# Graph build of a four-layer GNN and FFN kernel: part sums taken as rows in one float32 product, side work written between the tiles, and a new tail of l1_ffn

## Time and profile before

| What | us |
|---|---|
| median of 3 runs | 3308.21 (3299.77 to 3309.79) |
| the profiled execution | 3304.56 |
| its span | 3302.6 |
| build_graph's table | 0 to 29 |
| window loop of build_graph | 29 to 442 |
| finish_graph | 442 to 471 |
| end of l1_ffn, from L497 on | 1844.7 to 1884.2 |
| TensorE matmuls busy | 2694.3 (82%) |
| VectorE busy | 1684.6 (51%) |

### The profile page before, as it was taken

How to read it: one execution, slowest core, us unless ns; L and a number is a source line. 1 busy time by engine, 2 the same in 40 slices (tenths; PEclk the granted TensorE clock), 3 DMA queues, 4 the chain that set the end, 5 groups by cost and what they waited for, 6 DMA issues and landing times. The chain is left out here.

```text
span 3302.6 us, 41258 instructions
## 1 busy us (share of the span) xinstructions
PE 2694.3 (82%) x12659; PEld 1893.4 (57%) x12660; DVE 1684.6 (51%) x3356; ACT 943.7 (29%) x2087; POOL 278.1 (8%) x273
## 2 busy tenths in 40 slices
PE   5888869995899985999588599977877579999774
PEld 3555545564687754666365266665644457777452
DVE  6777752134788835444533722242132458886343
ACT  1222230103567741111111022211111236777110
POOL 0000000000000001444000000002210000000031
PEclk9999979997899987999798799978978789999777
DMA  3000042202000005898413130033232110000354
GB/s 104 1 0 0 0 135 46 60 0 63 19 19 22 16 9 168 293 301 285 114 46 129 27 75 13 0 109 112 90 91 52 44 34 19 19 18 13 81 143 110
DMA packets 113512, 237.85 MB, mean 72 GB/s; under 512 B 32500, under 2 KB 33860, under 8 KB 112130
## 3 DMA queue, kind: packets, MB, share of 16 engines
q10 hardware_dynamic: 41158, 110.67, 11.8%
q1 hardware_dynamic: 47932, 97.96, 9.9%
q0 software_dynamic: 24320, 27.90, 2.9%
HBM read 189.78 MB, written 52.58 MB: 73 GB/s over the span
## 5 line engine op out<-in xcount | busy, mean ns | idle before, releaser
L1050 DVE TENSOR_REDUCE mx<-ps 125x1 f32<-125x500 f32 (+1 forms) x480 | 273.9, 589 | 56.6 <-PE ps L820 40.4
L243 PE MATMUL ps<-onehot_src,onehot_dst 125*128 x1200 | 258.4, 354 | 41.5 <-DVE onehot_dst L219 17.4
L945 ACT ACTIVATE probs_hi<-ps 125x500 fp32r<-125x500 f32 (+1 forms) x480 | 255.7, 533 | 124.2 <-DVE probs_lo L1002 76.9
L218 DVE TENSOR_SCALAR onehot_src<-iota,src_f 125x1250 f16 x400 | 218.1, 545 | 108.1 <-PE ps L243 95.1
L1002 DVE TENSOR_TENSOR probs_lo<-x,probs_hi 125x1250 fp32r<-125x1250 f32 x160 | 240.8, 1505 | 35.7 <-ACT x L947 32.1
L947 ACT ACTIVATE x<-ps 125x500 f32<-125x500 f32 (+1 forms) x480 | 258.9, 539 | 0.0
L1694 DVE COPY yb<-ps 78x512 f32<-78x512 f32 (+1 forms) x100 | 68.9, 689 | 323.2 <-PE ps L1631 323.2
L243 PEld LDWEIGHTS ps<-onehot_src,onehot_dst 125*128 x1200 | 121.0, 102 | 172.4 <-issue 117.8
L1631 PE MATMUL ps<-w2s,hT 128*78 128x512 f32 (+1 forms) x480 | 216.7, 598 | 1.8 <-ACT hT L1656 1.8
L820 PE MATMUL ps<-K_hi_lo,Q_hi_twice 128*125 128x500 f32 (+1 forms) x480 | 181.2, 384 | 23.2 <-DVE mx L1050 18.1
L828 PE MATMUL ps<-Q_hi_twice,K_hi_lo 128*125 128x500 f32 (+1 forms) x480 | 179.5, 374 | 17.9 <-ACT Q_lo_max L935 5.1
(11 more groups left out here) (368 smaller groups left out, 4773.6 us busy)
## 6 DMA issues: line engine op xcount, KB each, us to landing
room<-in_L_ffn_w_p ACTq DMA_DIRECT2D x63, 512.0 KB, 4.7
w2s<-in_L_ffn_w ACTq DMA_DIRECT2D x63, 512.0 KB, 6.0
G<-c_spill ACTq DMA_DIRECT2D x2, 5859.4 KB
tv<-in_L_ffn_tv_W_p SPq DMA_DIRECT2D x2, 4096.0 KB
w_spill<-W SPq DMA_DIRECT2D x5, 1171.9 KB
c_spill<-CT ACTq DMA_DIRECT2D x1, 5859.4 KB
slabs<-w_spill SPq DMA_DIRECT2D x10, 585.9 KB
w1s<-in_L_ffn_w_p ACTq DMA_DIRECT2D x5, 1024.0 KB, 4.9
```

The costliest lines, as they stand in the source:

```text
L218: v.tensor_scalar(ohs[:, slot, :].rearrange("p o n -> p (o n)"), io16[:, 0:N], sF[:, bass.ds(tile, 1)], None, ALU.is_equal)
L243: mm_ = pe.matmul(ps[:, 3 * half + c, 0:cn], ohd[:, slot, :].rearrange("p o n -> p (o n)"), ohs[:, slot, c0:c0 + cn].rearrange("p o n -> p ...
L945: act.activation(PH[:, t % 2, c0:c0 + cn], ps[0:P, ST + n, 0:cn], ACT.Exp, scale=SCALE).then_inc(p_hi, 1)
L1050: v.tensor_reduce(mx[:, t, n:n + 1], ps[0:P, SQ + cc % 2, 0:cn], AX.X, ALU.max)\
```

## The change

1. HEAD = 7 tiles of each window are written out; then come runs of RUN = 2. With the same edges a window takes 9 or 11 tiles, 380 in all.
2. `sel_parts` becomes the stationary operand and `parts` (the old `stage`) the moving one: three float32 matmuls for a window (500, 500, 250 columns) give the rows of counts (partitions 0 to 31) and of weights (32 to 63) of the window. ScalarE copies them to `Crow` and `Wrow`, with the row sums of the counts as a by-product (`accum_out`, to `deg`). They stand between the written-out tiles two windows later, behind tiles 0, 2 and 4.
3. Per group ten PE transposes turn `Crow` into columns of CT, behind tiles of the next group's windows 2 and 3. ScalarE issues the write of `Wrow` to `w_spill` for each group.
4. The loop is written as a first group, a loop of 4 rounds with two groups each, and a last group; then the rest of the side work.
5. finish_graph goes; a small block works out the degree columns from `deg`.
6. In l1_ffn VectorE adds b2b to xn beside columns_product too; a new `blend` multiplies the identity with xn into the same PSUM sums, takes statistics, scales and adds to x row tile by row tile, and takes the statistics of x, so that l2_gnn's norm_rows need not.

```diff
-RUN = 4
-ETP = ET + RUN
+HEAD = 7
+RUN = 2
+ETP = ET + HEAD + RUN
...
-        stage = sb("stage", [128, 2, N])
+        parts = sb("parts", [128, 2, N])
+        Crow, Wrow = (sb(n, [P, 2, N]) for n in ("count_rows", "weight_rows"))
+        deg = sb("deg", [P, 3, T])
...
+                s.did(v.tensor_scalar(ti[:, 0:1], tl[:, 5:6], float(HEAD), float(RUN - 1 - HEAD), ALU.max, ALU.add))
...
+        AUX = 6
+        SRC = ((0, 4), (4, 4), (8, 2))
+        def sums(j, those):
+            return [("sum", j, c) for c in those]
+        def turns(*those):
+            return [("turn", None, q) for q in those]
+        def three_sums(w, n, j):
+            return {(w, 2 * c): (n + c, sums(j, (c,))) for c in range(3)}
+        PIECES = {"first": {**three_sums(2, 0, 0), **three_sums(3, 3, 1)},
+                  "body": {**three_sums(0, 0, 2), **three_sums(1, 3, 3), **three_sums(2, 6, 0), **three_sums(3, 10, 1),
+                           (2, 6): (9, turns(0)), (3, 5): (13, turns(1)), (3, 6): (14, turns(2))},
+                  "end": {(0, 0): (0, sums(2, (0, 1, 2)) + sums(3, (0, 1, 2)) + turns(0, 1, 2))}}
+        ROWS_DONE = 5
+        def chunk(i, where, n):
+            return n if where == "first" else i * 15 + (n - 9)
+        def aux(i, parity, where, q, j, slot, do_sum, do_turn):
+            first, pieces = PIECES[where].get((j, slot), (0, ()))
+            for n, (what, jj, c) in enumerate(pieces, first):
+                m, bank = chunk(i, where, n), (n + (1 if where != "first" and parity == 0 else 0)) % 2
+                if what == "turn":
+                    do_turn(i, 1 - parity, where, m, bank, c)
+                elif jj >= 2:
+                    do_sum(i - 1, jj, 1 - parity, None, m, bank, c)
+                else:
+                    do_sum(i, jj, parity, q, m, bank, c)
+        def schedule(eng, group):
+            group(0, 0, "first", 0)
+            with eng.Fori(0, T // 2 - 1) as q:
+                group(q * 2 + 1, 1, "body", q)
+                group(q * 2 + 2, 0, "body", q + 1)
+            group(T - 1, 1, "body", T // 2 - 1)
...
+                        for t in range(HEAD):
+                            onehots(first + t, before + t, base)
+                        with v.Fori(0, runs) as r:
                             for h in range(RUN):
-                                onehots(first + RUN * q + (1 + h), before + RUN * q + (1 + h), base)
+                                onehots(first + RUN * r + (HEAD + h), before + RUN * r + (HEAD + h), base)
...
+                def sum_parts(g, j, parity, q, m, bank, c):
+                    (c0, cn), h = CH[c], j % 2
+                    pe.wait_ge(aux_out, m * 2 + 2)
+                    if c == 0:
+                        pe.wait_ge(parts_ready, (g * WPT + j) * 2 + 6)
+                    pe.matmul(ps[0:64, AUX + bank, 0:cn], sel[:, :], parts[:, h, c0:c0 + cn], start=True, stop=True)\
+                        .then_inc(aux_done, 1)
+                def turn_counts(i, parity, where, m, bank, c):
+                    s0, sn = SRC[c]
+                    pe.wait_ge(aux_out, m * 2 + 2)
+                    if c == 0:
+                        pe.wait_ge(aux_out, chunk(i, where, ROWS_DONE) * 2 + 6)
+                    for t in range(sn):
+                        mm_ = pe.transpose(ps[0:P, AUX + bank, P * t:P * t + P],
+                                           Crow[:, parity, P * (s0 + t):P * (s0 + t) + P], k.ident[0:P, 0:P])
+                    mm_.then_inc(aux_done, 1)
+                def group(i, parity, where, q):
                     for j in range(WPT):
                         w = i * WPT + j
                         first, runs, before = window(pe, w)
...
+                        pe.wait_ge(parts_ready, w * 2 + 2)
+                        for t in range(HEAD):
+                            add_tile(j % 2, before + t, t == 0)
+                            aux(i, parity, where, q, j, t, sum_parts, turn_counts)
+                        with pe.Fori(0, runs) as r:
                             for h in range(RUN):
...
+                                add_tile(j % 2, before + RUN * r + (HEAD + h), False)
                         pe.drain().then_inc(window_summed, 1)
...
+                schedule(pe, group)
+                aux(T, 0, "end", None, 0, 0, sum_parts, turn_counts)
...
+                def stage_window(i, j, where):
+                    h = j % 2
                     act.wait_ge(window_summed, i * WPT + j + 1)
...
+                    if where != "first" or j >= 2:
+                        last = {0: 2, 1: 5, 2: 8, 3: 12} if where != "first" else {2: 2, 3: 5}
+                        act.wait_ge(aux_done, chunk(i, where, last[j]) + 1)
+                    act.activation(parts[:, h, 0:1000].rearrange("p (c n) -> p c n", c=2),
+                                   ps[:, 3 * h:3 * h + 2, 0:500], ACT.Copy).then_inc(parts_ready, 1)
+                    act.activation(parts[:, h, 1000:N], ps[:, 3 * h + 2, 0:250], ACT.Copy).then_inc(parts_ready, 1)
+                def take_sums(g, j, parity, q, m, bank, c):
+                    c0, cn = CH[c]
                     n = min(WIN, P - j * WIN)
...
+                    act.wait_ge(aux_done, m + 1)
+                    if j == 0 and c == 0:
+                        act.wait_ge(w_out[parity], q * 32 + 32)
+                    act.activation(Crow[WIN * j:WIN * j + n, parity, c0:c0 + cn], ps[0:n, AUX + bank, 0:cn], ACT.Copy,
+                                   accum_out=deg[WIN * j:WIN * j + n, c, bass.ds(g, 1)]).then_inc(aux_out, 1)
+                    act.activation(Wrow[WIN * j:WIN * j + n, parity, c0:c0 + cn], ps[WIN:WIN + n, AUX + bank, 0:cn],
+                                   ACT.Copy).then_inc(aux_out, 1)
+                    if j == WPT - 1 and c == 2:
+                        act.wait_ge(aux_out, m * 2 + 6)
+                        for r0, rn in ((0, 120), (120, 5)):
+                            act.dma_start(w_spill[bass.ds(g * P + r0, rn), :], Wrow[r0:r0 + rn, parity, :])\
+                                .then_inc(w_out[parity], 16)
+                def take_counts(i, parity, where, m, bank, c):
+                    s0, sn = SRC[c]
+                    act.wait_ge(aux_done, m + 1)
+                    act.activation(CT[:, s0:s0 + sn, bass.ds((i - 1) * P, P)],
+                                   ps[0:P, AUX + bank, 0:P * sn].rearrange("p (t n) -> p t n", n=P), ACT.Copy)\
+                        .then_inc(aux_out, 2)
+                def group(i, parity, where, q):
                     for j in range(WPT):
...
+                        for t in range(HEAD):
+                            aux(i, parity, where, q, j, t, take_sums, take_counts)
+                        stage_window(i, j, where)
+                schedule(act, group)
+                aux(T, 0, "end", None, 0, 0, take_sums, take_counts)
+                for s_ in w_out:
+                    act.wait_ge(s_, 32 + 32 * (T // 2))
+        cols = sb("cols", [P, 3, T])
+        deg1, root_done, end_steps = sem("deg1"), sem("root_done"), sem("end_steps")
+        with nc.Block() as block:
+            @block.scalar
+            def _(act):
+                act.wait_ge(deg1, 1)
+                act.activation(cols[:, 1, :], cols[:, 0, :], ACT.Sqrt).then_inc(root_done, 1)
+            @block.vector
+            def _(v):
+                s = Steps(v, end_steps)
+                s.did(v.tensor_reduce(cols[:, 2, :], deg[:, :, :].rearrange("p c t -> p t c"), AX.X, ALU.add))
+                s.wait()
+                v.tensor_scalar(cols[:, 0, :], cols[:, 2, :], 1.0, None, ALU.add).then_inc(deg1, 1)
+                s.did(v.tensor_scalar(cols[:, 2, :], cols[:, 2, :], 1.0, None, ALU.max))
+                s.wait()
+                v.reciprocal(k.inv_deg[:, :], cols[:, 2, :])
+                v.wait_ge(root_done, 1)
+                v.reciprocal(k.dinv[:, :], cols[:, 1, :])
...
-            norm_rows(nc, k, x, xn, xT, beside=[weights(0), (cols[:, :, :, :], a["L2_gnn_bgb"])],
+            norm_rows(nc, k, x, xn, xT, have_stats=True, beside=[weights(0), (cols[:, :, :, :], a["L2_gnn_bgb"])],
...
+        def add_biases(v):
+            v.tensor_tensor(xn[:, :, :], xn[:, :, :], b2b[:, :].unsqueeze(1).broadcast_to([P, T, D]), ALU.add)
+            return v.tensor_tensor(x[:, :, :], x[:, :, :], lnbb[:, :].unsqueeze(1).broadcast_to([P, T, D]), ALU.add)
         columns_product(nc, k, [(W1m, xT, C)], FC, lambda act, m, ch, n, psum:
                         act.activation(hT[:, m, ch[0]:ch[0] + ch[1]], psum, ACT.Relu, bias=b1m[:, m:m + 1]),
-                        vector=lambda v: v.tensor_tensor(x[:, :, :], x[:, :, :],
-                                                         lnbb[:, :].unsqueeze(1).broadcast_to([P, T, D]), ALU.add))
-        rows_product(nc, k, [(hT, W2m, FC)], b2b, add_rows(xn), xn, biased)
-        steps = sem("steps")
-        norm_rows(nc, k, xn, xn, have_stats=True)
-        with nc.Block() as block:
-            @block.vector
```

(50 more changed lines are left out.)

111 lines of the change are left out of this document (19 added, 92 removed).

## The result

The changed kernel took 3280.78 us (median of 6 runs, 3274.02 to 3288.02) where the one before took 3305.93 (6 runs, 3299.77 to 3310.25): a ratio of 0.9924, interval 0.9909 to 0.9939, so 25 us faster. Forecast were 53 us and a time of 3255, range 3232 to 3286. The profiled execution after took 3278.42 us, its span 3276.6 against 3302.6.

What follows compares the result with a forecast made beforehand. PE was taken to set the pace in the window loop. Gains of 27 (loop), 21 (build tail), 3 (l1_ffn's tail) and 2 (l2_gnn) made 53 us, giving a time of 3255, range 3232 to 3286.

Steps and rivals of the forecast that it cites:

- What the sums covered: Window loop: sums between tiles cost 2.1 us and hide the sequencer, each window idles 1.5; 8.8 us windows, loop gain 27.
- The write collides with nothing: Window loop: ScalarE's w_spill writes, about 1 us a group to issue, meet no other DMA during 90 to 430 us.
- The clock: Window loop: the clock dip in each group may go with add_parts' 64-column products, worth 5 us at most.
- The smaller terms of the loop: Window loop: transposes 13 us, extra tiles and steps back 17, two windows without sums -3, no idle after the last -2.
- ScalarE and VectorE: Window loop: ScalarE busy 5 of 8.8 us a window, VectorE 7.7, both under PE; bank emptying costs nothing.
- Rival B, the sequencer: Window loop: address work keeps PE at 0.70 us a tile or slower; loop gain 0, time 3282; chance 0.16.
- Rival C, code that no longer stays: Window loop: larger body makes engines reload instructions at steps back; 25 us, time 3280; chance 0.08.
- Tail of the build: Graph build after the window loop: 36 us become about 15, gain 21, bounds 17 and 24.
- l1_ffn's tail and l2_gnn: blend bound by VectorE at 3.2 us a tile, gain 3; l2_gnn without ten statistics and G sooner, gain 2.

Runs made afterwards that it cites:

- e1: Changed kernel with both 500-column sums of a window behind tile 0 and the third behind tile 4: 3276.01 us, ratio 0.9917 to the kernel before.
- e4: Changed kernel with each sum cut into two halves, the second behind the next tile: 3328.79 us, ratio 1.0073 to the kernel before.
- e10: Changed kernel with the sums' selector 128 columns wide (its 64 columns twice), still float32: 3265.04 us, ratio 0.9867 to the kernel before.
- e5: Changed kernel with selector and parts in bf16, each product issued four times for equal column passes: 3296.36 us, ratio 0.9974 to the kernel before.
- e3: Changed kernel with two sums right behind the previous window's drain, ahead of the entry's reading, the third behind tile 2: 3221.33 us, ratio 0.9755.
- the cover: Changed kernel's two 500-column sums moved behind the previous window's drain, before the entry's reading: 3221.33 us; with moved write 3225.13, with 128-column selector 3217.54.

## Why the prediction was wrong

The sign was right, and half of the gain was missing. By its own steps:

**What the sums covered: wrong, and this is the step that failed.** It reads "9 x 0.53 = 4.8, end of the last matmul 0.3, sums 2.1, idle 1.5: 8.7 us". The 2.1 for the sums was taken from products among their like the earlier trace rows and is right for the column passes; but each sum is a change of stationary width and back, 0.24 us, and three a window make it 2.84. Over the 114 stretches of the loop that is 27 of the 30 us by which the loop ended late (437.8 for 407.5). e1 and e4 show that the price goes by stretches, e10 that it hangs on the width of the stationary tile (and with it on the number of partitions written, which can't be changed apart), e5 that it is not the data type. Within that step of the working the 0.53 between tiles and the pause of 1.3 to 1.5 held. It also saw the pause as a price to pay; e3 shows that the sums could have covered it, for the greater part of 62 us.

**"The write collides with nothing": wrong.** I looked for a transfer that it could meet, not for a sequencer's read. It adds 5.5 us in the passages, measured. Whether it also brings dips stays open, since the same loop had six in one execution and three in another.

**The clock: wrong in half.** I let the dips go with the 64-column products of add_parts. Six remained, and make about 9 us (the first eight steps of all forty windows take 302 us, and without dips they would take 293). The 64-column products of add_parts are gone there, so they aren't needed for a dip. All six stand behind a pause of 2.0 us or more, though not every such pause has one. The three kernels with the cover have no dip in the loop, the kernels with pauses have two to nine in one profiled execution each. That fits the pauses as the cause; a kernel with pauses and without dips wasn't made.

**The smaller terms of the loop** were kinder than forecast: transposes 10 us for 13, two more tiles and a step back 1.1 in eight of ten windows (12 us in all) for 1.7 (17), the passages with the last tile 92 us, the write's 5.5 among them, for some 96 (forty times 8.8 less the 6.4 of steps and sums, less 2). Dearer were the first two windows, without sums (2 us), the steps at 0.54 for 0.53 (1.5 us), and the start (1 us later).
27 + 9 - 3 - 5 - 3 + 2 + 1.5 + 1 = 30, rounded.

**ScalarE and VectorE: right.** No sum waited for a bank in the loop; VectorE stayed ahead.

**Rival B, the sequencer: no.** Steps without a sum stayed at 0.53 to 0.55 with the new address work.

**Rival C, code that no longer stays: its mechanism is there, its price isn't.** The DMA view of 90 to 430 us, empty before, shows (packets, MB, share):

```profile
q14 instruction: 23, 0.19, 0.2%
q8 instruction: 4, 0.07, 0.1%
```

At the outer loop's steps back VectorE stands still for some 4 us while two 8 KB packets come:

```profile
144.68 0.55 DVE L263 TENSOR_SCALAR onehot_src<-iota,src_f 125x1250 f16 x1 [4.08 <-PE ps L292]
```

The row names PE, but the tile whose slot it waits for was multiplied by 141.1, 3.6 us before. VectorE leads PE by 7 us, and is still 4 us ahead at the next window's first tile. PE's passage there is 2.7 us instead of 2.2, at three such places. The 16 KB packets of q8 come at 106.6, 125.3, 146.6 and 414.4 us, in the body's first turn and at the last group, and none in the three turns between. This agrees with the rule of the Trainium skill (Runtime: NRT & Kernel Launch, Instruction fetch mechanics) as I had read it, VectorE's body does not fit and PE's stays, if q14 brings VectorE's code and q8 PE's, which the moments suggest and nothing names.

**Tail of the build: right.** 15.5 us for 15; gain 20.5 for 21. Between the build's end and l1_ffn's tail another 5 us came that I had not forecast: 1.3 at the change of block, 2.5 up to the first products (ScalarE's issue of c_spill takes 2.15 us for 3.48), the rest in small steps through the layers. What causes them wasn't tried.

**l1_ffn's tail and l2_gnn: right within 1 us.** VectorE 3.19 us a tile for 3.2; G issued 5.1 us after the block's start for 5.5; first G product 53.0 for 53; together 3.9 us net for 5, since PE started it at the lower clock.

The whole: -3.3 + 20.5 + 5 + 3.9 = 26, the difference of the spans. The error is one of the loop, -30, against +5 elsewhere.

## What to carry to other kernels

A product put between products with a stationary tile of another width need not cost its column passes alone: look at whether its weight load, and that of the product behind it, start ahead; if they don't, give it the same stationary width, even with columns that nobody reads, or join the stretches. Side work belongs where PE would stand still (behind a drain, ahead of an entry's reading), not where it is busy: the same sums cost 24 us among the tiles and at the pause they let the loop end 38 us sooner than with the old sums (375.2 against 413.4), dips included. And when a schedule is written out by hand, check what the sequencer reads from SBUF against the DMAs issued just before, and compare the number of dips in two executions of the same loop before putting a change of it down to anything.

## What the runs showed of the hardware

- Going from a 128-column stationary tile to a 64-column one and back cost 0.24 us, in float32 and in bf16 alike, by stretch and not by product; between 128 and 125 columns nothing (four transposes 0.42 us).
- A sequencer's read of one number from SBUF took 0.30 us. With the 0.6 MB write of the weight rows issued 0.8 us before it took up to 1.71, with 1.4 us between 1.05 to 1.21, with 2.4 us 0.50 to 0.59, and in the kernel with the cover, from 2.7 us on, 0.30 to 0.35 (once 0.64), packets of the write still in flight.
- A load of 5.9 MB issued together with one of 1 MB, and not behind its landing, put off work that needed the latter by 8.6 us, and the issue itself took 3.51 us instead of 1.20.
- The same loop, in two executions of two kernels that differ only behind it, had six dips of the granted clock and three.
